# Decoder layer with a mixture of Kronecker experts: the up layer in 64x64 tiles, a second activation for the down router

## What is computed

```python
def kmoe(x_flat, W_router, A, B, scale, bias, d_in1, d_in2, d_out1, d_out2, top_k):
    logits = x_flat @ W_router.T
    vals, idx = jax.lax.top_k(logits, top_k)          # top_k = 2 of 64 experts
    probs = jax.nn.softmax(vals, axis=-1)
    xs = x_flat.reshape(-1, d_in1, d_in2)
    Y = jnp.einsum('nkoi,nij,nkpj->nkop', A[idx], xs, B[idx])
    out = jnp.einsum('nkop,nk->nop', Y, probs).reshape(-1, d_out1 * d_out2)
    return out * scale + bias

h = kmoe(x_flat, W_up, A_up, B_up, scale_up, bias_up, 32, 32, 64, 64, 2)
h = jax.nn.gelu(h, approximate=False)
y = kmoe(h, W_down, A_down, B_down, scale_down, bias_down, 64, 64, 32, 32, 2)
```

## Time and profile before

| | us |
|---|---|
| median of 3 runs | 1493.66 |
| lowest, highest | 1488.32, 1494.98 |
| the profiled execution | 1486.11 |
| its span (first to last instruction) | 1484.2 |
| busy: PE, PEld, DVE, ACT, POOL | 1404.7, 1093.2, 1060.1, 905.3, 728.5 |
| mean granted TensorE clock | 0.979 of full |

### The profile page before, as it was taken

How to read it: one execution, slowest core, us unless ns; L and a number is a source line. 1 busy time by engine, 2 the same in 40 slices (tenths; PEclk the granted TensorE clock), 3 DMA queues, 4 the chain that set the end, 5 groups by cost and what they waited for, 6 DMA issues and landing times.

```text
span 1484.2 us, 50675 instructions
## 1 busy us (share of the span) xinstructions
PE 1404.7 (95%) x16466; PEld 1093.2 (74%) x16466; DVE 1060.1 (71%) x4099; ACT 905.3 (61%) x3062; POOL 728.5 (49%) x2385
## 2 busy tenths in 40 slices
PE   6899999999999999999999999999999999998765
PEld 5677787877778787787877778787877778776644
DVE  1367678786867878686887868688786868878453
ACT  2457576665757666575766657576675757666431
POOL 3123465464646546464654546465454646544353
PEclk9899999999999999999999999999999999999786
DMA  9100000000000000000000000000000000000000
GB/s 294 36 15 2 16 2 16 10 16 9 3 23 3 16 10 16 9 3 23 2 16 10 16 9 8 19 2 16 10 16 9 12 15 2 17 2 9 2 9 9
DMA packets 18584, 27.22 MB, mean 18 GB/s; under 512 B 2193, under 2 KB 17170, under 8 KB 18066
## 3 DMA queue, kind: packets, MB, share of 16 engines
q1 hardware_dynamic: 18322, 23.98, 5.4%
HBM read 19.78 MB, written 4.19 MB: 16 GB/s over the span
## 4 chain that ended last, share of the span: by engine, by line
PE 82%; DVE 9%; issue 4%; POOL 1%; ACT 1%; DVEq 1%; POOLq 0%; ACTq 0%
PE G L842 8%; PE P L704 8%; PE P L672 7%; PE PT L724 6%; PE G L800 6%; PE P L683 5%; PE P L661 5%; PE F L831 4%; PE X L746 4%; PE X L759 4%; PE PT L759 4%; PE S L718 3%; PE G L871 3%; PE F L858 3%; PE S L716 2%
## 5 line engine op out<-in xcount | busy, mean ns | idle before, releaser
L337 POOL COPY chosen_up<-experts 32x128 f32 x1024 | 327.6, 344 | 240.0 <-PE G L842 115.5
L350 POOL COPY chosen_dn<-experts 64x64 f32 x1024 | 215.1, 265 | 106.6 <-issue 49.3
L571 ACT ACTIVATE probs<-probs,neg_max 128x128 f32<-128x128 f32 (+1 forms) x512 | 226.1, 446 | 7.8 <-DVE neg_max L978 6.5
L337 ACT COPY chosen_up<-experts 32x128 f32 x512 | 119.0, 292 | 120.9 <-PE G L842 114.5
L978 DVE CUSTOM_DVE_ANT_0 probs<-S,distance 128x128 f32<-128x128 f32 (+1 forms) x512 | 152.3, 354 | 15.7 <-PE S L718 11.9
L842 PE MATMUL G<-chosen_up,W 128*64 128x256 f32 x1024 | 137.9, 389 | 9.0 <-DVE W L1096 5.8
L724 PE MATMUL PT<-ident,probs 128*128 128x128 f32 x768 | 131.8, 281 | 8.0 <-ACT probsT L578 3.1
L996 DVE TENSOR_TENSOR probs<-probs,rinv 128x768 f32<-128x768 f32 x128 | 124.4, 972 | 4.4
L704 PE MATMUL P<-xnT,wq 128*128 128x256 f32 x512 | 124.7, 388 | 0.8 <-ACT xnT L524 0.8
L578 ACT COPY probsT<-PT 128x384 f32<-128x384 f32 x128 | 61.4, 480 | 101.9 <-PE PT L724 69.3
L683 PE MATMUL P<-wv,ctxT 128*128 128x256 f32 x512 | 122.8, 383 | 0.0
(11 more groups left out here) (130 smaller groups left out, 3016.9 us busy)
## 6 DMA issues: line engine op xcount, KB each, us to landing
x<-in_x SPq DMA_DIRECT2D x16, 256.0 KB, 2.6
ctxT<-in_ctxT SPq DMA_DIRECT2D x16, 256.0 KB, 2.6
out<-x2b SPq DMA_DIRECT2D x16, 256.0 KB, 2.2
r_dn<-in_r_dn SPq DMA_DIRECT2D x1, 2048.0 KB, 15.2
experts<-in_experts_up SPq DMA_DIRECT2D x2, 1024.0 KB, 22.0
wk<-in_xWk SPq DMA_DIRECT2D x1, 1024.0 KB
wo<-in_xWo SPq DMA_DIRECT2D x1, 1024.0 KB
wv<-in_xWv SPq DMA_DIRECT2D x1, 1024.0 KB, 7.7
```

Of the source, the lines that this page charges most:

```text
L337: last = copy(dst, src.rearrange("p (m c) -> p m c", m=2))
L350: last = copy(dst, src.rearrange("p (m c) -> p m c", m=2))
L571: act.activation(probs[:, e % 4, lo:hi], probs[:, e % 4, lo:hi], ACT.Exp, bias=neg_max[:, e % 4, rt:rt + 1], scale=-1.0, accum_out=rsum[:, ...
```

## The change

Up layer: a slot holds a pair and there are 4 slots. Each token has its own 128 columns in it (64 of A, 64 of B) and its half of the rows (0 to 63 for the first 4 tokens of a pair, 64 to 127 for the other 4), with the two choices in the two blocks of 32 rows. So both products work on tiles of 64 rows, 64 weight columns and 64 moving columns, one token and both choices at a time: 8 matmuls for `first` and 8 for `second` (4 and 4 before). The sum over the two choices is now inside one matmul. `own` doubles to 128 x 2048, `xn3T` is laid out by token, and the slots are not zeroed any more. `weigh` and `pre` keep their sizes.

Down router: `gelu` first writes a second, transposed copy `hT` (128 rows; the tokens of a column are contiguous) with four activations of 64 x 1024 read from `h` with a step of 64 elements, and then activates `h` in place as before. `router_dn` waits for the four, `dn_first.0` for the two. `logits_dn` has 32 matmuls with 128 rows, 64 weight columns (tokens), 64 moving columns, on two alternating column halves of G. `r_dn` is half as large (1 MB), `fold` adds two blocks, not four.

ORDER is written anew as a whole. Around the router it reads now:

```diff
-pv.7@2 pre.6@3 weigh.7@3 keep_out.7@2 second.7@3 pre.7@3 gelu@3 root@1 x1.0@1 ln2_stats.0@1 x1.1@1 ln2_stats.1@1
-wo.0@2 load_x ln2_root@1 router_dn@3 logits_dn.0@3 logits_dn.1@3 logits_dn.2@3 logits_dn.3@3 ln2.0@1 ln2.1@1 turn2@1
-xnT2@1 x2_bias@3 part@3 fold@3 top_dn@3 wo.1@2 ln1_stats x2.0@2 q.0@1 gap_dn@3 weights_dn@3 ln1_root x2.1@2
+weigh.6@3 turn_b.7@2 second.6@3 choose_dve.15@3 catch_b.7@2 pre.6@3 first.7@3 weigh.7@3 pv.7@2 keep_out.7@2 second.7@3
+pre.7@3 x1.0@1 x1.1@1 ln2_stats.0@1 v_keep.1@1 wo.0@2 wo.1@2 ln2_stats.1@1 ln2_root@1 ln2.0@1 ln2.1@1 turn2@1
+x2_bias@3 gelu@3 router_dn@3 logits_dn.0@3 xnT2@1 load_x ln1_stats x2.0@2 ln1_root x2.1@2 logits_dn.1@3 ln3_stats@2
+logits_dn.2@3 ln1 x1_bias@1 logits_dn.3@3 part@3 fold@3 top_dn@3 gap_dn@3 q.0@1 q_keep.0@1 weights_dn@3 ln3_root@2
```

The rest, cut to its core:

```diff
-UP_SLOTS, DN_SLOTS = 5, 4
+UP_SLOTS, DN_SLOTS = 4, 4
...
-            dst = own[n * D1:(n + 1) * D1, :].rearrange("j (g n r c i) -> j n i c g r", n=2, r=4, c=CT, i=4)
-            src = xn3T[il * D1:(il + 1) * D1, :, :].rearrange("j c (r g n) -> j n c g r", n=UP_TOK, r=4)
-            return dst[:, n % 2, il], src[:, n]
+            half, k = divmod(n, TOPK)
+            dst = own[n * D1:(n + 1) * D1, :].rearrange("j (v p k a i) -> j k i v p a", v=UP_PAIRS, p=UP_TOK, k=TOPK, i=4)
+            src = xn3T[il * D1:(il + 1) * D1, :, :].rearrange("j a (v h p) -> j h v p a", h=2, p=UP_TOK)
+            return dst[:, k, il], src[:, half]
...
             for unit in units:
                 n, k = divmod(unit, TOPK)
-                a, b = (k * UP_TOK + n) * F1, A_UP + k * F1
-                dst = to[n * D1:(n + 1) * D1, a:a + F1]
-                dst = bass.AP(dst.tensor, dst.offset, [dst.ap[0], [b - a, 2], [1, F1]])
-                src = experts_up[n % 2][:, bass.ds(held[g % LOADED, unit], 2 * F1)]
-                last = copy(dst, src.rearrange("p (m c) -> p m c", m=2))
+                row = half * F1 + k * D1
+                last = copy(to[row:row + D1, n * 2 * F1:(n + 1) * 2 * F1],
+                            experts_up[k][:, bass.ds(held[g % LOADED, unit], 2 * F1)])
...
             def gelu(c):
-                half = UP_PAIRS // 2 * UP_TOK * F1
+                wait_g(act, "second", UP_PAIRS - 1, c)
+                after(act, parts_done, c)
+                for half in range(2):
+                    for oh in range(2):
+                        src = h[half * F1:(half + 1) * F1, :].rearrange("p (n h o) -> p h o n", h=2, o=F1 // 2)[:, oh]
+                        dst = hT[oh * F1:(oh + 1) * F1, :, half * TOKENS // 2:(half + 1) * TOKENS // 2]
+                        act.activation(dst, src, ACT.Gelu).then_inc(hT_ready, 1)
+                cols = UP_PAIRS // 2 * UP_TOK * F1
+                act.wait_ge(hT_ready, at(c, 4, 4))
                 for i in range(2):
-                    wait_g(act, "second", (i + 1) * UP_PAIRS // 2 - 1, c)
-                    cols = slice(i * half, (i + 1) * half)
-                    act.activation(h[:, cols], h[:, cols], ACT.Gelu).then_inc(h_ready, 1)
+                    part = slice(i * cols, (i + 1) * cols)
+                    act.activation(h[:, part], h[:, part], ACT.Gelu).then_inc(h_ready, 1)
...
             def logits_dn(c, part):
-                size = F1 // ROUTER_CUTS
+                size = F1 // 2 // ROUTER_CUTS
                 for o in range(part * size, (part + 1) * size):
-                    for half in range(2):
-                        rows, to = slice(half * F1, (half + 1) * F1), half * F1 + o % 2 * 32
-                        tokens = h[rows, :].rearrange("p (n o) -> p o n", o=F1)[:, o, :]
-                        mm = pe.matmul(G[to:to + 32, 0:EXPERTS], tokens, r_dn[rows, o, :],
-                                       start=(o < 2), stop=(o >= F1 - 2))
+                    to = o % 2 * F1
+                    mm = pe.matmul(G[to:to + F1, 0:EXPERTS], hT[:, o, :], r_dn[:, o, :],
+                                   start=(o < 2), stop=(o >= F1 // 2 - 2))
...
-                for j in (0, 1):
-                    g = 2 * v + j
+                for p in range(UP_TOK):
+                    m, b = v * UP_TOK + p, (2 * p + 1) * F1
                     for half in range(2):
                         rows = slice(half * F1, (half + 1) * F1)
-                        mm = pe.matmul(F[rows, j * B_UP:(j + 1) * B_UP], own[rows, g * F1:(g + 1) * F1],
-                                       chosen_up[g % UP_SLOTS][rows, A_UP:A_UP + B_UP], start=True, stop=True)
+                        mm = pe.matmul(F[rows, p * F1:(p + 1) * F1], own[rows, m * F1:(m + 1) * F1],
+                                       chosen_up[v % UP_SLOTS][rows, b:b + F1], start=True, stop=True)
...
-                n = UP_TOK * F1
-                for k in range(TOPK):
-                    for j in (0, 1):
-                        w = j * B_UP + k * F1
-                        mm = pe.matmul(G[j * F1:(j + 1) * F1, 0:n], W_up[v % 2][:, w:w + F1],
-                                       chosen_up[(2 * v + j) % UP_SLOTS][:, k * n:(k + 1) * n], start=(k == 0), stop=(k == TOPK - 1))
+                for p in range(UP_TOK):
+                    a = 2 * p * F1
+                    for half in range(2):
+                        rows = slice(half * F1, (half + 1) * F1)
+                        mm = pe.matmul(G[rows, p * F1:(p + 1) * F1], W_up[v % 2][rows, p * F1:(p + 1) * F1],
+                                       chosen_up[v % UP_SLOTS][rows, a:a + F1], start=True, stop=True)
```

More of the change, by code:

```diff
@@ L95 @@
+catch_a.4@1 turn_b.4@1 v.0 store@3 exp.5@1 cumulate v_keep.3@1 cross.1 second.1@2 first.2@2 choose_pool.9@2
+catch_b.4@1 choose_act.8@2 scale.5@1 weigh.2@2 pre.1@2 mask.6@1 pv.4@1 turn_a.5@1 second.2@2 product_q first.3@2 k.0
+choose_act.9@2 weigh.3@2 v_keep.0 choose_act.10@2 pre.2@2 catch_a.5@1 turn_b.5@1 choose_dve.9@2 choose_dve.10@2
+keep_out.4@1 choose_dve.11@2
 """
```

107 lines of the change are left out of this document (52 added, 55 removed).

## The result

| | before | after | forecast |
|---|---|---|---|
| median, us | 1491.45 (1488.32 to 1494.98) | 1468.32 (1465.30 to 1471.34) | 1418 |
| ratio | | 0.984, interval 0.981 to 0.988 | |
| profiled execution, span | 1486.11, 1484.2 | 1465.30, 1463.4 | 1418, 1416 |
| mean granted clock | 0.979 | 0.958 | |
| a steady turn | 86.3 | 84.6 | 81.7 |

A forecast was written before the change was run, and what follows sets the result against it. PE was taken to bound the kernel; a turn of 86.4 - 7.0 (products, router) + 1.8 (wait) + 0.5 (fold) = 81.7 us, over 14 turns 66 us less, plus some 2 us from half-empty turns, gave 1418 us, range 1380 to 1456.

The forecast's parts named there:

- What bounds the kernel: Whole kernel: PE is short of time, busy 95% of the span, only about 1.2 us idle in an 86.4 us turn.
- Parts 1 and 2: Up layer's second and first products on PE, in 64x64 tiles: 3.4 and 0.3 us saved a batch.
- Rival C: Row tiles exclude each other in banks F and G, 75 ns an instruction: slower, 1586 us; chance 0.04.
- Part 3: Down router on PE: 64 instructions at 36 ns, 2.3 us instead of 5.66; 3.3 us saved, range 0.9 to 3.6.
- part 5: Fold behind the router: it waits for DVE's copy of the logits with nothing between, costing 0.5 us.
- Part 4: Four added strided ACT activations ahead of the router, 2.0 us each: PE waits 1.8 us a batch.
- rival A: The added activations read with a step for free, so no 1.8 us wait: 1389 us; chance 0.22.
- Part 6: Hidden work: doubled copies and activations take ACT to about 67 us and DVE to 67.4 a turn, covered by PE.
- Other moves zero: The whole order written anew: its other moves cost zero, bounded by minus 1 and plus 3 us a turn.
- The sum: Steady turn 86.4 - 7.0 + 1.8 + 0.5 = 81.7 us, 4.7 less; 14 turns give 66 us; 1418 us.
- half-empty turns: The two turns before the last batch's lone end: some 2 us of gain.
- Rival B: New order leaves PE waits, as DVE and ACT answer a faster up layer: 2.5 us a turn, 1453 us; chance 0.22.

The follow-up runs named there:

- straight_read: After, with the four added activations reading neighbouring elements in line, not with a step (output not the reference's); 1418.53 us, 0.9511.
- token_major: After, with hT laid out by token: activations copy runs of 32 in line, the router reads its weights with a step; 1448.22 us, 0.9724.
- Filler: After, with 8 matmuls that nobody reads put between turn2 and the router's wait; 1453.98 us, 0.9744.
- straight128: straight_read with the second product's tiles on 128 rows again (output not the reference's); 1425.61 us, 0.9548.
- up_oldorder: Before, with the whole up layer of the change, but the router, activation and order of before; 1474.72 us, 0.9895.
- early: After, with the transposed activations of pairs 0 to 3 moved earlier in the turn, in eight activations of 64x512; 1502.26 us, 1.0084.
- k1_cover: After, with projection k.1 moved between turn2 and the router on PE, its copy behind xnT2 on ACT; 1446.13 us, 0.9707.
- second128: up_oldorder with the second product's tiles on 128 rows again (output not the reference's); 1473.53 us, 0.9874.

## Why the forecast was wrong

By the steps of the prediction:

- **What bounds the kernel**: PE, right for before. In after it is still PE, but for one place in a turn, where it is ACT.
- **Parts 1 and 2** (forecast -3.7 us a turn): -3.6, right. A first product ahead of a second takes 0.52 us in after for 16 instructions, 32 ns each; the means over all seams are 0.57 for the first product and 0.55 for the second. Rival C is rejected by that: 64x64 tiles in both row halves work at once with one bank as their target. The rule of the Trainium skill (TensorEngine Tiling (Array Packing), Restrictions and Gotchas) behind that rival is not borne out here.
- **Part 3 and part 5**, router and fold together: the forecast comes to 3.1 us (2.3, the 0.5 of waiting for DVE's copy, and 0.3 for the fold itself). At the full clock it is 2.7 (2.4 until the fold's start and 0.3, in straight_read), in after 3.6. The term that the prediction lacks is the clock.
- **Part 4**: the activation, 2.0 us against 1979 ns, right; rival A is rejected, and straight_read and token_major show that the step on the reading side is the cause. The wait was 2.2 for 1.8, as PE arrives 0.3 us sooner. The step that failed is that I took the wait for all that it costs. Filler shows 1.2 us more a turn from the clock behind it: 0.9 in the router, 0.1 in the fold, 0.2 in the projections behind them.
- **Part 6**: the copies were priced rightly (ACT 68.9 and DVE 68.0 us in the turn from 777.4 to 862.0, forecast 67 and 67.4). "Other moves zero" failed by +1.9 us a turn, the largest miss. 0.2 of it is the low clock, which reaches the projections behind the fold (68.5 and not 68.7 us in straight_read). 0.3 goes with the new tile of the second product (68.2 in straight128). The other 1.4 is there when the second product has its old tile back, so it is the order's, or that of waits behind a faster up layer. Which of the two is argued and not shown. Taking for each pair of neighbouring steps the least time that it took in any turn, the untouched steps go from 66.1 to 67.7 us; what lies above these least times grows only from 0.7 to 1.1, and 0.2 of that is the clock. So most of it looks like dearer neighbours that the order gives, and not like waits: the k projections go from 7.0 to 7.4 us a turn, pv from 6.0 to 6.5, the turned probabilities from 6.5 to 7.3. A projection with 8 instructions of 256 columns takes from 1.73 us, ahead of its own kind or of turned probabilities in most places, to 1.82 and 1.92, ahead of steps with smaller tiles, and the new order has more of such seams. A least time can hide a wait that comes in every turn, though: in up_oldorder, by the same count, it took in 0.6 us of the waits for DVE.
- **The sum**: forecast -4.7 a turn, measured -1.7. The 3.0 between them are 1.9 (the untouched steps, 0.2 of it the clock), 0.6 (router and fold, at the lower clock), 0.4 (the longer wait) and 0.1 (parts 1 and 2). 14 turns make 42 of the 47 us that the span missed by. The other 5 are in the ends, where I expected 2 us of gain from the half-empty turns and zero elsewhere, and 3 were lost.
- **Rival B** had nearly the size (2.5 us a turn) without the mechanism: in after the short waits grew by 0.2 us. What it describes happened in the old order: up_oldorder has 1.0 us of new waits for DVE in the untouched steps and 0.4 more in a first product. The new order took these waits away; in their place its untouched steps seem to have dearer neighbours. That DVE and ACT are dense around the up layer shows in early too, where a move of one step costs more than it wins.

Open: how the 1.4 us divides between neighbours and waits, and which seams carry how much. The kernel before in the new order, with nothing else changed, would tell and was not run. Moving other projections into the wait, in part, was not tried, nor k1_cover with a better place for the Fourier copy.

## What to carry to other kernels

A wait on the bound engine costs more than its length when the clock falls behind it (3.4 us for 2.2 here): price it with the rows of the slow clock, and put work there, useful if there is some (k.1, 22 us), else none that anybody reads (14 us). When an operand is transposed by a strided copy, both ends of it have a price, and the one to load is the engine that has slack at that place, not in the mean. When an order is written anew, don't price its moves at zero: sum PE's time from start to start of neighbouring steps, for steps that nobody edits change too (1.4 us a turn here, most of it, it seems, by what stands next to them). And when a step gets faster and the order stays, ask what answers it: in the old order 1.0 us of the gain went into waits for DVE.

## What the runs showed of the hardware

- A wait of 2.2 us on PE, once in 85 us, was followed by 3.4 us at 1.2 GHz in 10 of 14 turns; in the other 4 turns the same wait was followed by none. Waits of 0.5 us (k1_cover) and the filled wait left it at 2.4 GHz: their granted clock from 350 to 1200 us is 1.00, that of after 0.98.
- ACT reads 64 x 1024 f32 with a step of 256 bytes in 1979 ns, in line or in runs of 32 elements in 1056 ns: 0.90 ns more per element. The Trainium skill (SBUF — State Buffer, in its note on 16-byte lines) says that each access to a new line pays; the trace agrees, with that figure for ACT's reads.
- A weight load of 64 f32 columns with a step of 128 bytes takes 220 ns (token_major), in line 143 (straight_read, full clock), and the router, in which nothing else differs, 4.5 us for 64 instructions instead of 2.4.
- Tiles of 64x64 in both row halves, written to one bank: 16 instructions in 0.52 us. A change of tile shape between neighbours: 0.06 to 0.1 us on PE in the seams where only the shape was edited (second128, straight128). A projection takes 1.73 to 1.92 us by what stands behind it.
